# An SSM mixer layer with a dense and low-rank layer behind it on one core: x turned on VectorE and through DRAM instead of on TensorE, and the carried sum moved to GpSimd

## The chip, the cores and the metric

The kernel runs on one core of one Trainium2 chip. The metric is the device time of one execution in microseconds.

## What is computed

Input `x` is (2, 512, 512): batch, sequence, features. The reference, cut to what matters here:

```python
proj = einsum('bsd,ed->bse', layernorm(x), in_proj_w)       # gate 8192, x B C 10240, dt 128
hBC  = silu(causal_conv4(proj[..., INTER:INTER + CONV_DIM]) + conv_b)
hs, Bm, Cm = split(hBC)                                       # 128 heads of 64; 8 groups of 128 states
dt   = clip(softplus(dt + dt_bias), 0, 100);  xch = hs * dt[..., None]      # in chunks of 128 tokens
Y_diag = einsum('bzlhn,bzshn,bhzls,bzshp->bzlhp', Cc, Bc, L, xch)
states = einsum('bzlhn,bhzl,bzlhp->bzhpn', Bc, decay_states, xch)           # and carried over the chunks
Y_off  = einsum('bzlhn,bzhpn,bhzl->bzlhp', Cc, prev, exp(A_cum))
y = Y_diag + Y_off + hs * D;   g = y * silu(gate);   gg = g * rsqrt(mean(g * g) + EPS) * norm_w
x = x + einsum('bsi,oi->bso', gg, out_proj_w)
x = x + layernorm(x) @ W.T + b + sum_e probs_e * (layernorm(x) @ A_e.T) @ B_e.T
```

## The kernel before

The inner width of 8192 is cut into 64 units of 128 features, that is, two heads; eight units share one group's B and C. Features lie on the partitions after the projection, tokens on the free axis (two batches of 512 tokens). `body(g, last)` of each engine is a written-out loop over the eight units `j` of a group, and `k` counts the units. The engines are kept in step by counting semaphores, and each runs its instructions in the order written.

One unit on TensorE, in this order: the later half of the previous output product (`later_outs`), the projection of the next unit's x into `x_bank` (L778 to L780, each product in three parts of high and low halves), `states` for both batches (L786), `diagonal` (L797), the projection of the next unit's gate into `g_bank`, `carry` (L804), the first half of the output product (L835 to L837), in units 4 and 5 the projection of the next group's B or C, and `turn_hs` (L812): eight transposes that bring the next unit's x from features to tokens on the partitions, into `head_bank`.

```python
def turn_hs(k, s, b):
    pe.wait_ge(hs_ready, k + 1)
    reached(pe, carry_scaled, BATCH * (k - 1) + b + 1)
    for c in range(CHUNKS):
        mm = pe.transpose(head_bank[b][:, c * P:(c + 1) * P], hs[:, s, b, c * P:(c + 1) * P], ident[:])
    mm.then_inc(turned, 1)
```

The causal convolution of x has four taps: `tap0` is ScalarE's (L1033, `x_bank` to `hs`), the three others VectorE's (L1199), then Silu on ScalarE (L1045) makes `hs_ready`. VectorE's order in a unit: `to_heads` (L1278, the turned x times dt into `xdt`), `add_outs` and `score` in turns, `y_low_part` (L1215), in units 1 to 3 from the second group on `normed_out` (L1304), the first tap, `carried_state` (L1240, L1245), two taps, `skip` (L1261, which makes `y`), `carry_part` (L1256, both batches), `add_carry` (L1268, both batches, which adds the carried part to `y` and signals `y_sum`), and `add_outs`. In units 5 and 6 three taps of B or C (L1208) stand near its start, and in unit 7 `keep_bc` (L1285) ahead of `y_low_part`.

GpSimd multiplies `y` by the gate (`gated`, L1462, one instruction per batch, after `y_sum`) and `xdt` by the decay (`decayed`, L1469, after `xdt_ready`, and `states` on TensorE waits for it), and makes low halves (L1448, L1487) and the sum of squares (L1456). SyncE's queue issues every load: weights (L674), `out_raw` (L678), `scores` (L682) and, last in a unit, `grown_rows` (`load_grown`, L689, two DMAs per batch), which wait for that batch's `y_sum` because `carry_part` and `add_carry` use `grown_rows`.

## Time and profile before

| | |
|---|---|
| time, median of 3 runs | 1605.14 us (1604.95 to 1605.45) |
| the profiled execution, span | 1605.0 us |
| TensorE busy | 1583.5 us (99%) |
| VectorE busy | 1264.2 us (79%) |
| ScalarE busy | 1163.1 us (72%) |
| GpSimd busy | 700.7 us (44%) |
| DMA moved | 162.37 MB, 101 GB/s on average |

The page gives the span of the one profiled execution, and no time of it beside that. Busy shares are averages over the span; the order of things inside a unit is read from the timeline, where times count from the span's start. A TensorE matmul's duration contains its pipeline, so the step from one start to the next says what it costs.

### The profile page before, as it was taken

How to read it: one execution, taken by the hardware profiler on the slowest of the kernel's cores; microseconds unless marked ns; L12 is line 12 of the kernel's file. 1: busy time of each engine (PE TensorE's matmuls, PEld its weight loads, DVE VectorE, ACT ScalarE, POOL GpSimd, SP SyncE). 2: the span in 40 equal slices, each digit the busy share in tenths (PEclk: the TensorE clock that was granted, in tenths of full speed). 3: DMA queues.
4: the chain of work that ended last, by engine and by line, in shares of the span. 5: the costliest groups of instructions: out<-in, count | busy, mean ns of one | idle time of the engine just before them, and what ended most of it. 6: DMA issues, size and time to landing. Idle time of an engine off the chain costs nothing.

```text
span 1605.0 us, 26714 instructions
## 1 busy us (share of the span) xinstructions
PE 1583.5 (99%) x9576; PEld 1346.1 (84%) x9576; DVE 1264.2 (79%) x1984; ACT 1163.1 (72%) x2027; POOL 700.7 (44%) x535
## 2 busy tenths in 40 slices
PE   7899999999999999999999999999999999999998
PEld 5688888888888888888888888888888888888887
DVE  6687777877778777887778877787877878788787
ACT  5887667776777677777687766777677767777753
POOL 2155444453444454354453544445344445435550
PEclk9999999999999999999999999999999999999999
DMA  4542322332323233332232232233232323223211
GB/s 151 192 145 86 122 89 83 112 112 73 112 97 114 73 109 95 98 106 92 99 108 97 86 122 89 83 112 112 73 112 99 113 73 109 99 92 112 93 44 53
DMA packets 86916, 162.37 MB, mean 101 GB/s; under 512 B 23040, under 2 KB 39424, under 8 KB 86528
## 3 DMA queue, kind: packets, MB, share of 16 engines
q1 hardware_dynamic: 86784, 160.66, 30.8%
q8 instruction: 77, 1.26, 0.3%
q14 instruction: 55, 0.45, 0.1%
HBM read 154.84 MB, written 5.77 MB: 100 GB/s over the span
## 4 chain that ended last, share of the span: by engine, by line
PE 97%; DVE 1%; ACT 1%; issue 0%; DMA 0%; SPq 0%; DVEq 0%; ACTq 0%
PE g_bank L778 10%; PE g_bank L780 9%; PE g_bank L779 9%; PE d_bank L797 7%; PE x_bank L778 7%; PE x_bank L780 7%; PE x_bank L779 7%; PE head_bank L786 5%; PE head_bank L804 5%; PE x_bank L836 4%; PE x_bank L837 4%; PE x_bank L835 4%; PE d_bank L837 4%; PE d_bank L835 4%; PE d_bank L836 4%; PE head_bank L812 3%
## 5 line engine op out<-in xcount | busy, mean ns | idle before, releaser
L1448 POOL TENSOR_TENSOR w_low<-raw,w_high 128x512 fp32r<-128x512 f32 x139 | 179.8, 1294 | 553.5 <-ACT w_high L1011 553.5
L1199 DVE SCALAR_TENSOR_TENSOR hs<-x_bank,cols,hs 128x1022 f32<-128x1022 f32 x189 | 241.6, 1278 | 129.7 <-ACT hs L1033 127.5
L1021 ACT ACTIVATE scores<-scores,tables 128x128 f32<-128x128 f32 x1024 | 312.4, 391 | 0.0
L1462 POOL TENSOR_TENSOR y<-y,gate 128x512 f32<-128x512 f32 x128 | 185.4, 1467 | 198.8 <-DVE y L1268 198.8
L1033 ACT ACTIVATE hs<-x_bank,cols 128x1024 f32<-128x1024 f32 x63 | 75.9, 1204 | 269.9 <-PE x_bank L780 269.9
L778 PE MATMUL g_bank<-x_high,w_high 128*128 128x512 f32 x624 | 250.8, 402 | 0.0
L779 PE MATMUL g_bank<-x_low,w_high 128*128 128x512 f32 x624 | 243.2, 390 | 0.0
L780 PE MATMUL g_bank<-x_high,w_low 128*128 128x512 f32 x624 | 243.1, 390 | 0.0
L778 PE MATMUL x_bank<-x_high,w_high 128*128 128x512 f32 x504 | 196.3, 390 | 0.1
L780 PE MATMUL x_bank<-x_high,w_low 128*128 128x512 f32 x504 | 196.1, 389 | 0.0
L779 PE MATMUL x_bank<-x_low,w_high 128*128 128x512 f32 x504 | 196.1, 389 | 0.0
L1231 DVE TENSOR_TENSOR scores<-scores,bc 128x1024 f32<-128x1024 f32 x128 | 169.0, 1327 | 4.3 <-ACT scores L1026 4.3
L778 PEld LDWEIGHTS g_bank<-x_high,w_high 128*128 128x128 f32 x624 | 117.0, 188 | 33.4 <-issue 11.0
L1469 POOL TENSOR_TENSOR xdecay<-xdt,tables 128x384 f32<-128x384 f32 x128 | 109.0, 873 | 78.4 <-DVE xdt L1278 78.4
L780 PEld LDWEIGHTS g_bank<-x_high,w_low 128*128 128x128 f32 x624 | 117.1, 188 | 25.3
L1026 ACT ACTIVATE scores<-scores 128x1024 f32<-128x1024 f32 x128 | 135.8, 1062 | 2.6
L779 PEld LDWEIGHTS g_bank<-x_low,w_high 128*128 128x128 f32 x624 | 117.2, 188 | 22.4 <-issue 0.2
L1456 POOL TENSOR_TENSOR square_sum<-square_sum,gate 128x1024 f32<-128x1024 f32 x55 | 133.0, 2419 | 3.3 <-DVE scores L1231 2.9
L1245 DVE SCALAR_TENSOR_TENSOR state<-state,chunk_tab,head_bank 128x64 f32<-128x64 f32 x512 | 121.0, 278 | 9.1
L797 PE MATMUL d_bank<-scores,xdt 128*64 128x128 f32 x2048 | 126.1, 276 | 0.0
L1256 DVE TENSOR_TENSOR grown_rows<-head_bank,grown_rows 128x384 f32<-128x384 f32 x128 | 71.4, 557 | 64.4 <-PE head_bank L804 57.3
L797 PEld LDWEIGHTS d_bank<-scores,xdt 128*64 128x64 f32 x2048 | 110.5, 137 | 7.9 <-issue 0.2
(211 smaller groups left out, 3433.3 us busy)
## 6 DMA issues: line engine op xcount, KB each, us to landing
scores<-sums_dram SPq DMA_DIRECT2D x128, 512.0 KB, 4.8
raw<-w_in SPq DMA_DIRECT2D x144, 256.0 KB, 2.9
grown_rows<-grown_dram SPq DMA_DIRECT2D x256, 96.0 KB, 2.8
out_raw<-w_out SPq DMA_DIRECT2D x64, 256.0 KB, 3.4
mixed<-x SPq DMA_DIRECT2D x8, 256.0 KB, 5.1
out<-mixed SPq DMA_DIRECT2D x8, 256.0 KB, 2.0
table_dram<-table SPq DMA_DIRECT2D x2, 768.0 KB, 5.3
tables<-table_dram SPq DMA_DIRECT2D x30, 48.0 KB, 2.7
```

What stands on the lines that cost most here:

```text
L778: pe.matmul(to, w_high[:, slot, k], x_high[:, b, k], start=(k == 0), stop=False)
L779: pe.matmul(to, w_high[:, slot, k], x_low[:, b, k], start=False, stop=False)
L780: mm = pe.matmul(to, w_low[:, slot, k], x_high[:, b, k], start=False, stop=(k == KT - 1))
L797: mm = pe.matmul(d_bank[r * HEAD_DIM:(r + 1) * HEAD_DIM, b, c * P:(c + 1) * P], xdt[:, b, c, r], scores[:, s, b, r, c], start=True, stop=True)
L835: pe.matmul(to, y_high[:, q, b, at], out_high[:, q], start=(i == 0), stop=False)
L1021: op = s.activation(at, at, ACT.Relu, bias=col[:, r, c:c + 1], scale=-1.0)
L1026: s.activation(scores[:, q % 2, b], scores[:, q % 2, b], ACT.Exp, scale=-1.0).then_inc(exp_ready, 1)
L1199: v.scalar_tensor_tensor(out=hs[:, q % 2, :, i:], in0=x_bank[:, :, 0:SEQ - i], scalar=cols[:, q, TAPS - 1 - i:TAPS - i], in1=hs[:, q % 2, ...
L1231: v.tensor_tensor(at, at, bc[:, b].rearrange("p c l -> p (c l)").unsqueeze(1) .to_broadcast([P, PAIR, SEQ]), ALU.mult).then_inc(scores_rea ...
L1448: pool.tensor_tensor(w_low[:, slot], raw[:, slot], w_high[:, slot].bitcast(F32), ALU.subtract)\
L1456: pool.tensor_tensor(square_sum[:], square_sum[:], gate[:, q % 2], ALU.add).then_inc(square_added, 1)
L1462: pool.tensor_tensor(y[:, b], y[:, b], gate[:, q % 2, b], ALU.mult).then_inc(y_ready, 1)
```

## The change

The x of every unit but the first is no longer turned on TensorE. VectorE transposes `hs` in blocks of 32x32, one instruction per batch (`turn_blocks`), the result is stored to `blocks_dram`, one DMA per batch (`store_blocks`), and four DMAs per batch of 32 partitions each read it back so that the blocks too are in transposed places (`load_heads`). `to_heads` multiplies this `blocks` tile by dt; since the order of the features inside a head's 64 is now by halves of 32, the dt table is held twice, as two of four kinds. `to_heads` stands after the scores in VectorE's order and not at the unit's start. `add_carry` is GpSimd's, ahead of each batch's `gated`. `bias_high` and `bias_low` lie in the tiles of `x_low` and `x_high`, and their making waits for the last projection. The core of the diff:

```diff
@@ -19,6 +19,9 @@
 KT = HID // P
 UNITS = INTER // GROUPS // P
 PAIR = P // HEAD_DIM
+BLOCK = 32
+KINDS = 4
+QUARTERS = P // BLOCK
 GH = HEADS // GROUPS
 HALF = UNITS // 2
 ALL = GROUPS * UNITS
...
@@ -156,7 +160,7 @@
         big = lambda name: sb(name, [P, BATCH, CHUNKS * P])
         dense, wd = sb("dense", [P, KT, HID]), sb("wd", [P, KT, HID])
         sums, grown = big("head_sums"), big("head_grown")
-        table = sb("table", [P, BATCH, 2 * GROUPS, 3, GH // 2 * CHUNKS])
+        table = sb("table", [P, BATCH, 2 * GROUPS, KINDS, GH // 2 * CHUNKS])
         la, lb = sb("la", [P, ER, HID]), sb("lb", [P, ER, HID])
         xn = sb("xn", [P, 2, HID])
         wdt = sb("wdt", [P, KT, P])
...
@@ -398,9 +402,14 @@
             def table_of(i):
                 b, kind = TABLES[i]
                 s.wait_ge(table_turned, i + 1)
-                s.activation(table[:, b, :, kind].rearrange("p g (h c) -> p c g h", c=CHUNKS),
-                             bank[4 + i % 2].rearrange("p (c g h) -> p c g h", c=CHUNKS, g=2 * GROUPS),
-                             ACT.Copy).then_inc(table_ready, 1)
+                src = bank[4 + i % 2].rearrange("p (c g h) -> p c g h", c=CHUNKS, g=2 * GROUPS)
+                if kind == 0:
+                    twice = table[:, b, :, 0:2].rearrange("p g k (h z c) -> p z c g (k h)", z=2, c=CHUNKS)
+                    s.activation(twice[:, 0], src, ACT.Copy)
+                    s.activation(twice[:, 1], src, ACT.Copy).then_inc(table_ready, 1)
+                else:
+                    s.activation(table[:, b, :, 1 + kind].rearrange("p g (h c) -> p c g h", c=CHUNKS), src, ACT.Copy)\
+                        .then_inc(table_ready, 1)
 
             def first_tables(b):
                 s.wait_ge(table_ready, len(TABLES))
...
@@ -610,6 +619,7 @@
         square_sum, y = sb("square_sum", [P, BATCH, SEQ]), sb("y", [P, BATCH, SEQ])
         gate = sb("gate", [P, 2, BATCH, SEQ])
         out_raw = sb("out_raw", [P, 2, HID])
+        blocks = sb("blocks", [P, BATCH, QUARTERS, CHUNKS, BLOCK])
         xdt = sb("xdt", [P, BATCH, CHUNKS, PAIR, HEAD_DIM])
         c_feat, bc = sb("c_feat", [P, BATCH, SEQ]), sb("bc", [P, BATCH, CHUNKS, P])
         grown = grown_rows
...
@@ -660,6 +672,10 @@
 
         def table_of(kind, b, q):
             return tables[:, b, q // HALF, kind, PAIR * (q % HALF):PAIR * (q % HALF + 1)]
+
+        def dt_of(b, q):
+            twice = tables[:, b, q // HALF, 0:2].rearrange("p k h c -> p (k h) c")
+            return twice[:, QUARTERS * (q % HALF):QUARTERS * (q % HALF + 1)]
 
         (first_sync, first_stores, first_dense, first_gpsimd, first_tensor, first_scalar, first_vector,
          dense_ready) = first
...
@@ -688,6 +704,22 @@
                 for r in range(PAIR):
                     sp.dma_start(grown[r * HEAD_DIM:(r + 1) * HEAD_DIM, b].rearrange("p c l -> p (c l)"),
                                  rows[r, P:].partition_broadcast(HEAD_DIM)).then_inc(grown_in[b], 16)
+
+            def store_blocks(k):
+                for b in range(BATCH):
+                    sp.wait_ge(blocks_ready, BATCH * (k - 1) + b + 1)
+                    reached(sp, heads_in[b], 16 * QUARTERS * (k - 2))
+                    sp.dma_start(blocks_dram[BATCH * (k % 2) + b], blocks[:, b].rearrange("p j n f -> p (j n f)"))\
+                      .then_inc(blocks_stored[b], 16)
+
+            def load_heads(k):
+                for b in range(BATCH):
+                    sp.wait_ge(blocks_stored[b], 16 * k)
+                    turned_blocks = blocks_dram[BATCH * (k % 2) + b].rearrange("(q t) (j n) -> j t q n", t=BLOCK,
+                                                                               j=QUARTERS)
+                    for i in range(QUARTERS):
+                        sp.dma_start(blocks[i * BLOCK:(i + 1) * BLOCK, b].rearrange("p q n f -> p q (n f)"),
+                                     turned_blocks[i]).then_inc(heads_in[b], 16)
 
             def load_chunks(g, b, half):
                 at = slice(half * GH // 2, (half + 1) * GH // 2)
...
@@ -744,8 +776,10 @@
                     for at in splits[2:]:
                         load_weight(*at)
                     if ahead:
+                        store_blocks(ahead[2])
                         for b in range(BATCH):
                             load_grown(ahead[2], b)
+                        load_heads(ahead[2])
                     if last and j == UNITS - 1:
                         sp.wait_ge(b_turned, BATCH * GROUPS)
                         sp.dma_start(bias_row, bias.partition_broadcast(P)).then_inc(bias_in, 16)
...
@@ -782,6 +816,7 @@
 
             def states(k, b):
                 pe.wait_ge(xdecay_ready, BATCH * k + b + 1)
+                reached(pe, carry_scaled, BATCH * (k - 1) + b + 1)
                 for c in range(LATER):
                     mm = pe.matmul(head_bank[b][:, c * P:(c + 1) * P], b_tok[:, b, c],
                                    xdecay[:, b, c].rearrange("p r d -> p (r d)"), start=True, stop=True)
...
@@ -805,11 +840,10 @@
                                    c_feat[:, b, (c + 1) * P:(c + 2) * P], start=True, stop=True)
                 mm.then_inc(carried, 1)
 
-            def turn_hs(k, s, b):
-                pe.wait_ge(hs_ready, k + 1)
-                reached(pe, carry_scaled, BATCH * (k - 1) + b + 1)
+            def turn_first(b):
+                pe.wait_ge(hs_ready, 1)
                 for c in range(CHUNKS):
-                    mm = pe.transpose(head_bank[b][:, c * P:(c + 1) * P], hs[:, s, b, c * P:(c + 1) * P], ident[:])
+                    mm = pe.transpose(head_bank[b][:, c * P:(c + 1) * P], hs[:, 0, b, c * P:(c + 1) * P], ident[:])
                 mm.then_inc(turned, 1)
 
             def bc_of(b, to):
...
@@ -937,9 +971,6 @@
                         pe.wait_ge(gate_ready, BATCH * (k + 2))
                         for b in range(BATCH):
                             project(g, (NEXT_B, NEXT_C)[j - 4], b, g_bank[:, b])
-                    if ahead:
-                        for b in range(BATCH):
-                            turn_hs(k + 1, (j + 1) % 2, b)
                     if j == 0 and g > 0:
                         pe.wait_ge(square_added, (UNITS - 1) * g)
                         pe.wait_ge(gate_ready, BATCH * (k + 2))
...
@@ -1157,6 +1188,7 @@
                     if last and j == UNITS - 1:
                         s.activation(ident_r[:], ident[:], ACT.Copy)
                         s.wait_ge(bias_in, 16)
+                        s.wait_ge(projected, BATCH * TILES)
                         s.activation(bias_high[:], bias_row, ACT.Copy).then_inc(bias_high_ready, 1)
                         s.wait_ge(dense_in, 16)
                         for i in range(KT):
...
@@ -1261,23 +1293,31 @@
                 v.scalar_tensor_tensor(out=y[:], in0=hs[:, q % 2], scalar=d_col[:, q:q + 1], in1=d_bank[:],
                                        op0=ALU.mult, op1=ALU.add).then_inc(skip_added, 1)
 
-            def add_carry(k, b):
-                u = BATCH * k + b
-                v.wait_ge(carry_scaled, u + 1)
-                v.wait_ge(skip_added, k + 1)
-                v.tensor_tensor(y[:, b, P:], y[:, b, P:], grown[:, b].rearrange("p c l -> p (c l)"), ALU.add)\
-                 .then_inc(y_sum, 1)
+            def turn_blocks(k, i):
+
+                v.wait_ge(hs_ready, k + 1)
+                for b in range(BATCH):
+                    reached(v, blocks_stored[b], 16 * (k - 1))
+                    v.transpose(blocks[:, b], hs[:, i, b].rearrange("p (c j t) -> p j c t", j=QUARTERS, t=BLOCK))\
+                     .then_inc(blocks_ready, 1)
 
             def to_heads(g, q, k, b):
                 if q % HALF == 0:
                     v.wait_ge(tables_in[b][q // HALF], 16 * (g + 1))
-                v.wait_ge(turned, BATCH * k + b + 1)
                 reached(v, diag_done, BATCH * (k - 1) + b + 1)
                 reached(v, xdecay_ready, BATCH * (k - 1) + b + 1)
-                col = table_of(DT, b, q).rearrange("p r c -> p c r")
-                v.tensor_tensor(xdt[:, b], head_bank[b].rearrange("p (c r d) -> p c r d", c=CHUNKS, r=PAIR),
-                                col.unsqueeze(3).to_broadcast([P, CHUNKS, PAIR, HEAD_DIM]), ALU.mult)\
-                 .then_inc(xdt_ready, 1)
+                if k == 0:
+                    v.wait_ge(turned, b + 1)
+                    col = dt_of(b, q)[:, 0::QUARTERS // PAIR].rearrange("p r c -> p c r")
+                    v.tensor_tensor(xdt[:, b], head_bank[b].rearrange("p (c r d) -> p c r d", c=CHUNKS, r=PAIR),
+                                    col.unsqueeze(3).to_broadcast([P, CHUNKS, PAIR, HEAD_DIM]), ALU.mult)\
+                     .then_inc(xdt_ready, 1)
+                else:
+                    v.wait_ge(heads_in[b], 16 * QUARTERS * k)
+                    v.tensor_tensor(xdt[:, b].rearrange("p c r (h f) -> p (r h) c f", f=BLOCK),
+                                    blocks[:, b],
+                                    dt_of(b, q).unsqueeze(3).to_broadcast([P, QUARTERS, CHUNKS, BLOCK]), ALU.mult)\
+                     .then_inc(xdt_ready, 1)
 
             def keep_bc(g, src):
                 v.wait_ge(bc_product, BATCH * (g + 1))
...
@@ -1359,8 +1399,9 @@
                     k = UNITS * g + j
                     prev, now, ahead = (unit(g, last, j + i) for i in range(-1, 2))
 
-                    for b in range(BATCH):
-                        to_heads(g, j, k, b)
+                    if k == 0:
+                        for b in range(BATCH):
+                            to_heads(g, j, k, b)
                     if j == 1 and g > 0:
                         squares_of(g)
                     if k > 2:
...
@@ -1375,6 +1416,9 @@
                         add_outs(g, j - 1, (3,))
                     if scores_here:
                         score(g, j, k, 1)
+                    if k > 0:
+                        for b in range(BATCH):
+                            to_heads(g, j, k, b)
                     if j == UNITS - 1 and not last:
                         keep_bc(g + 1, g_bank)
                     if prev and ahead:
...
@@ -1392,17 +1436,15 @@
                         tap(2, *ahead)
                         tap(3, *ahead)
                         skip(j, k)
+                        turn_blocks(k + 1, (j + 1) % 2)
                         for b in range(BATCH):
                             carry_part(k, b)
-                        for b in range(BATCH):
-                            add_carry(k, b)
                     else:
                         y_low_part(prev[1], prev[2])
                         v.wait_ge(y_low_ready, k)
                         skip(j, k)
                         for b in range(BATCH):
                             carry_part(k, b)
-                            add_carry(k, b)
                     if k > 1:
                         add_outs(g, j, (0, 1))
                     else:
...
@@ -1455,6 +1497,13 @@
                 reached(pool, square_added, (UNITS - 1) * g + q - 1)
                 pool.tensor_tensor(square_sum[:], square_sum[:], gate[:, q % 2], ALU.add).then_inc(square_added, 1)
 
+            def add_carry(k, b):
+                u = BATCH * k + b
+                pool.wait_ge(skip_added, k + 1)
+                pool.wait_ge(carry_scaled, u + 1)
+                pool.tensor_tensor(y[:, b, P:], y[:, b, P:], grown[:, b].rearrange("p c l -> p (c l)"), ALU.add)\
+                    .then_inc(y_sum, 1)
+
             def gated(q, k, b):
                 u = BATCH * k + b
                 pool.wait_ge(y_sum, u + 1)
...
@@ -1489,6 +1538,7 @@
                     for at in splits[1:]:
                         low_part(*at)
                     for b in range(BATCH):
+                        add_carry(k, b)
                         gated(j, k, b)
 
             low_part(0, 3)
...
```

SyncE's queue, a plain unit of the kernel before, the named tiles being those of the loads above:

```order
L674 DMA raw<-w_in 128x512
L682 DMA scores<-sums_dram 128x1024 x2
L689 DMA grown_rows<-grown_dram 64x384 x4
L674 DMA raw<-w_in 128x512
L678 DMA out_raw<-w_out 128x512
```

The same place in the change:

```order
L690 DMA raw<-w_in 128x512
L698 DMA scores<-sums_dram 128x1024 x2
L712 DMA blocks_dram<-blocks 128x512 x2
L705 DMA grown_rows<-grown_dram 64x384 x4
L721 DMA blocks<-blocks_dram 32x4x128 x8
L690 DMA raw<-w_in 128x512
L694 DMA out_raw<-w_out 128x512
```

The two stores stand ahead of the four loads of `grown_rows`, the eight loads behind them and ahead of the next unit's weights.

VectorE, unit 1 of a group from its scores on, in the change (L1317 is `to_heads`, L1263 `score`, L1344 `normed_out`, L1301 `turn_blocks`, L1288 `carry_part`):

```order
L1263 TENSOR_TENSOR scores<-scores,bc 128x1024
L1317 TENSOR_TENSOR xdt<-blocks,tables 128x4x4x32 x2
L1247 SCALAR_TENSOR_TENSOR y_low<-y,cols,y_high 128x1024
L1363 RECIPROCAL g_rstd<-g_std 128x8
L1344 SCALAR_TENSOR_TENSOR mixed<-acc,g_rstd,mixed 128x512 x2
L1231 SCALAR_TENSOR_TENSOR hs<-x_bank,cols,hs 128x2x511
L1272 COPY state<-head_bank 128x128
...
L1293 SCALAR_TENSOR_TENSOR y<-hs,cols,d_bank 128x1024
L1301 STREAM_TRANSPOSE blocks<-hs 128x512 x2
L1288 TENSOR_TENSOR grown_rows<-head_bank,grown_rows 128x384 x2
L1340 TENSOR_TENSOR acc<-x_bank,acc 128x512 x2
```

`to_heads` has moved from the unit's start to behind the scores, ahead of `y_low_part`, the normed sums and the first tap; the two block transposes stand where the two `add_carry` stood behind `carry_part`, but ahead of it.

GpSimd, the end of a unit in the change (L1504 is `add_carry`, L1511 `gated`, L1518 `decayed`):

```order
L1490 TENSOR_TENSOR w_low<-raw,w_high 128x512
L1504 TENSOR_TENSOR y<-y,grown_rows 128x384
L1511 TENSOR_TENSOR y<-y,gate 128x512
L1504 TENSOR_TENSOR y<-y,grown_rows 128x384
L1511 TENSOR_TENSOR y<-y,gate 128x512
L1518 TENSOR_TENSOR xdecay<-xdt,tables 128x384 x2
```

Before, the four rows in the middle were one, `y<-y,gate` twice; the second batch's sum now comes behind the first batch's gate.

## Rows read from the trace of the kernel before

**Rows 1.** The page: busy us (share) xinstructions; shares of the chain that ended last, by engine

```profile
PE 1583.5 (99%) x9576; PEld 1346.1 (84%) x9576; DVE 1264.2 (79%) x1984; ACT 1163.1 (72%) x2027; POOL 700.7 (44%) x535
...
PE 97%; DVE 1%; ACT 1%; issue 0%; DMA 0%; SPq 0%; DVEq 0%; ACTq 0%
```

**Rows 2.** The waits: engine line <- released by: us in total, times, longest

```profile
DVE hs L1199 <- ACT hs L1033: 127.5, 62, 3.3
```

**Rows 3.** Timeline of ScalarE, `tap0`: start, us, line, [idle before <- releaser]

```profile
892.73 1.21 ACT L1033 ACTIVATE hs<-x_bank,cols 128x1024 f32<-128x1024 f32 x1 [4.80 <-PE x_bank L780]
...
914.73 1.21 ACT L1033 ACTIVATE hs<-x_bank,cols 128x1024 f32<-128x1024 f32 x1 [4.75 <-PE x_bank L780]
...
969.69 1.20 ACT L1033 ACTIVATE hs<-x_bank,cols 128x1024 f32<-128x1024 f32 x1 [4.75 <-PE x_bank L780]
...
993.57 1.21 ACT L1033 ACTIVATE hs<-x_bank,cols 128x1024 f32<-128x1024 f32 x1 [4.80 <-PE x_bank L780]
...
1016.21 1.20 ACT L1033 ACTIVATE hs<-x_bank,cols 128x1024 f32<-128x1024 f32 x1 [3.92 <-PE x_bank L780]
...
1039.12 1.20 ACT L1033 ACTIVATE hs<-x_bank,cols 128x1024 f32<-128x1024 f32 x1 [3.13 <-PE x_bank L780]
...
1083.26 1.21 ACT L1033 ACTIVATE hs<-x_bank,cols 128x1024 f32<-128x1024 f32 x1 [4.80 <-PE x_bank L780]
```

**Rows 4.** Timeline of TensorE around the transposes of one unit

```profile
905.00 0.39 PE L836 MATMUL x_bank<-out_low,y_high 128*128 128x512 f32 x1
905.23 0.39 PE L837 MATMUL x_bank<-out_high,y_low 128*128 128x512 f32 x1
905.46 1.03 PE L812 MATMUL head_bank<-ident,hs 128*128 128x128 f32 x8
906.25 0.48 PE L835 MATMUL d_bank<-out_high,y_high 128*128 128x512 f32 x1
```

**Rows 5.** Timeline of VectorE over the same units

```profile
890.56 2.07 DVE L1304 SCALAR_TENSOR_TENSOR mixed<-acc,g_rstd,mixed 128x512 f32<-128x512 f32 x3
893.97 1.28 DVE L1199 SCALAR_TENSOR_TENSOR hs<-x_bank,cols,hs 128x1022 f32<-128x1022 f32 x1 [1.34 <-ACT hs L1033]
...
900.10 1.27 DVE L1261 SCALAR_TENSOR_TENSOR y<-hs,cols,d_bank 128x1024 f32<-128x1024 f32 x1
902.25 1.23 DVE L1256 TENSOR_TENSOR grown_rows<-head_bank,grown_rows 128x384 f32<-128x384 f32 x2 [0.88 <-PE head_bank L804]
903.40 1.02 DVE L1268 TENSOR_TENSOR y<-y,grown_rows 128x384 f32<-128x384 f32 x2
...
906.27 1.28 DVE L1278 TENSOR_TENSOR xdt<-head_bank,tables 128x512 f32<-128x512 f32 x2
...
911.41 1.27 DVE L1215 SCALAR_TENSOR_TENSOR y_low<-y,cols,y_high 128x1024 fp32r<-128x1024 f32 x1
...
925.44 1.62 DVE L1268 TENSOR_TENSOR y<-y,grown_rows 128x384 f32<-128x384 f32 x2
...
990.39 1.23 DVE L1285 TENSOR_TENSOR bc<-g_bank,causal 128x1024 f32<-128x1024 f32 x1
```

**Rows 6.** Timeline of GpSimd in that unit

```profile
904.02 2.79 POOL L1462 TENSOR_TENSOR y<-y,gate 128x512 f32<-128x512 f32 x2 [3.33 <-DVE y L1268]
907.03 1.64 POOL L1469 TENSOR_TENSOR xdecay<-xdt,tables 128x384 f32<-128x384 f32 x2 [0.21 <-DVE xdt L1278]
```

**Rows 7.** Timeline of SyncE's DMA queue in that unit

```profile
903.97 2.37 SPq L689 DMA_DIRECT2D grown_rows<-grown_dram  x4
```

**Rows 8.** DMA issues (ns min/median/max) and landing: L674; L689 and its landing; a store

```profile
L674 SPq DMA_DIRECT2D raw<-w_in x138: 327/333/1240, 55.0 to 1489.4; - x138
...
L689 SPq DMA_DIRECT2D grown_rows<-grown_dram x252: 444/596/1980, 82.7 to 1543.5; - x126
...
DMA to landing us min/median/max: 2.5/2.8/5.1
...
sums_dram<-head_sums SPq DMA_DIRECT2D x2, 256.0 KB, 2.5
```

19 lines of the change are left out of this document (11 added, 8 removed).

## The prediction

> **What bounds the kernel now.** I began with the busy shares and the chain of work that ended last: TensorE is busy 99% of the span and carries 97% of that chain, no other engine over 79% [rows 1]. So time taken off TensorE is time off the kernel, as long as nothing else comes to hold it. The next view is the waits: VectorE waits 127.5 us in 62 units, about 2 us each, for ScalarE's `tap0`, which itself follows TensorE's projection [rows 2]. That is all the slack VectorE has, and in the units with normed sums it is less. The starts of `tap0` mark the units: a plain one takes 22.0 us (892.73 to 914.73), the two with a B or C projection 55.0 together, the next three 23.9, 22.6 and 22.9, and two more 44.1; eight units 190.5 [rows 3].
>
> **What TensorE loses.** Between two matmuls of the output product the starts lie 0.23 apart; with the eight transposes of L812 between them it is 905.23 to 906.25, so they take 0.8 us [rows 4]. They go in 63 units (only the first keeps them): 63 x 0.8 = 50 us, which with everything else hidden gives 1605.0 - 50 = 1555. The plain unit would be 21.2 us.
>
> **What comes in its place.** The transposes' result came from PSUM within a microsecond. Now it comes by this path, in a loop that closes once per unit: first tap, carried states, taps, skip, two block transposes, carry multiplication (VectorE); add, gate, add (GpSimd); the second batch's `grown` loads, eight block loads (SyncE's queue); landing; `xdt`, `y_low`, normed sums, and the next unit's first tap (VectorE). It is in one piece because `load_heads` stands behind both batches of `load_grown`, which wait for `y_sum` of both batches, and that sum is now GpSimd's, behind the first batch's gate multiplication. I add it up in the unit that starts at 893.97:
> - First tap to the end of skip: 893.97 to 901.3, 7.35 us (skip starts at 900.10 and takes 1.27, of which the next instruction overlaps some 0.07) [rows 5]. `hs` has its Silu by then.
> - Two transposes: no row shows this operation. The nearest are 128x512 on VectorE: `xdt`, two in 1.28 us [rows 5]. I take 1.25 for both; from below 0.6 (twice the rate), from above 2.5 (half the rate).
> - `grown` of batch 0: 1.23 for two, so 0.6 [rows 5]. Batch 1's is hidden behind GpSimd.
> - GpSimd: the gate multiplication of 128x512 takes 1.4 (two in 2.79), and `xdecay`, 384 wide, 0.82 (two in 1.64) [rows 6]. An add of 384 plain elements I take as 0.95; bounds 0.8 and 1.4. Add, gate, add with the handoffs: 3.35. On VectorE the two adds took 1.02 [rows 5], so VectorE's total stays as it was: 1.25 on, 1.0 off.
> - SyncE: four `grown` issues take 2.37 us, 0.59 each; batch 1's two: 1.2 [rows 7]. Then eight block loads, seven issues before the last one starts. Weight loads over 128 partitions issue in 0.33, `grown` over 64 partitions in 0.60 (medians) [rows 8]. A block load has 32 partitions and 512-byte pieces. The partial-partition row is nearest, so I take 0.6: 4.2 us. The low end is 0.33 (2.3 us), the high end 1.0 if pieces of 512 bytes queue up (7 us).
> - Landing: 2.8 us for `grown`, of 96 KB [rows 8]; a block load has 64 KB. I take 2.8; from below 2.2, from above 5, the longest of `grown` being 5.1.
> - `xdt` of batch 1 0.65, then `y_low` 1.2 [rows 5].
> The sum is 7.35 + 1.25 + 0.6 + 3.35 + 1.2 + 4.2 + 2.8 + 0.65 + 1.2 = 22.6 us, against TensorE's 21.2. The two stores are not in it: issued at about 902 and, with 2.5 us as for `sums_dram` [rows 8], landed by 905, while the SyncE queue stands at `y_sum` until about 906.5. Behind the eight loads wait the next weight and `out_raw` loads, whose data are used a unit later: nothing. ScalarE gets `y` about 1 us later, which comes out of the 3.1 to 4.8 us that it idles before `tap0` [rows 3]: nothing.
>
> The same loop closes through TensorE: `xdecay` of batch 1 ends 0.85 after its `xdt`, some 23.5 us after the start of `tap0`; TensorE would want it 0.7 after the start of `states`, at about 21.6. So the stall should stand in front of `states` (L786 of the kernel before).
>
> **The Trainium skill against this.** The row says 2.8 us for a small load. *DMA: Bandwidth & Descriptors*, section "Anatomy of one DMA", gives 2.0 us plus the bytes at 436 GB/s (for DMAs issued from GpSimd), an estimated 2.15 us for 64 KB; by it the loop would be 21.95 and the time 1613. The trace's row is longer, so I stay with the row. The same page's "Rules for kernel authors" says that transfers to separate parts of the partitions serialise and are better one transfer; it speaks against four loads where one would do, and no row here shows such a split by four.
>
> **Sum over eight units.** Each takes the larger of TensorE's time and the loop's.
> - Three units have normed sums, behind `xdt` in VectorE's queue and so in the loop: three of them take 2.07 us [rows 5], two with the reciprocal about 1.6. Times 24.2, 24.7, 24.7 (22.9, 22.05, 22.05 before).
> - The plain unit: 22.6 (22.0 before).
> - The two with extra projections: TensorE 27.5 - 0.8 = 26.7 each. The loop has 4 us to spare there.
> - The one after: the causal product, 1.23 [rows 5], follows `xdt`: 23.7 (23.9 before).
> - The last: 22.6 (22.6 before).
> Together 195.9 against 190.5, +5.4. Seven groups: +38. The first group has no normed sums and comes out even. The doubled `dt` table adds two ScalarE copies in the prologue and the last unit's sum goes over GpSimd, +1 together. **Forecast: 1605.0 + 39 = 1644 us.** The profiled span, 1605.0, is 0.1 under the median of the runs, 1605.14, so nothing is corrected. A measurement here can tell 0.2%, 3.2 us, from no change.
>
> **Rivals.**
> 1. *The loads issue fast.* At 0.43 each, the loop is 21.4: units of 23.0, 23.5, 23.5, 21.4, 26.7, 26.7, 23.1 and 21.9, together 189.8, so -0.7 in seven groups and -6 in the first: 1595. At 0.33 and 2.2 us to landing it is 20.1, the plain units are TensorE's, and the sum is 186.1: 1569. For it: the weight loads' 0.33 [rows 8]. Against: `grown`, with fewer pieces than these, takes 0.6. It decides below about 0.45 us per issue. This is the case on the other side. Chance 0.24.
> 2. *All hidden*, TensorE stays the bound everywhere: 1555. It needs the loop with normed sums under 21.2, 3.5 us less than the above. Chance 0.03.
> 3. *The transfers queue up* or the block transpose runs at half rate: a loop of 24.1 (1.5 more, say 0.8 us per load) gives 25.7, 26.2, 26.2, 24.1, 26.7, 26.7, 25.2 and 24.1, together 204.9: +14.4 in seven groups and 9 in the first, 1715. For it: GpSimd and VectorE read SBUF together, and one pair of adds took 1.62 instead of 1.02 [rows 5]. Chance 0.15.
> 4. *The change does not do what it says*, and the transposes stay: excluded by the instruction order, where they are gone from TensorE. A time within 0.2% comes about only where the loop happens to lie near 21.6: 0.08.
> The forecast itself, 1615 to 1680, has 0.50.
>
> **The numbers.** Slower by over 0.2%: the forecast's 0.50 and rival 3's 0.15, 0.65. Same: 0.08. Faster: 0.24 and 0.03, 0.27. The range takes in rival 1's low end nearly, 1575, and most of rival 3, 1700.
>
> **What would show it.** TensorE's busy time shorter by about 50 us and yet not the span: new idle time in front of `states`, released by GpSimd's `xdecay`, 1 to 3 us per unit, in five or six units of eight, and none in the two with extra projections. VectorE should wait for the landing of `blocks`. SyncE's queue should show eight issues of about 0.6 us that start right after `grown`. I am wrong if issues take 0.45 or less, if `heads_in` is met before VectorE gets to `xdt`, or if `states` waits for nothing.

## The result and the profile after

The changed kernel takes 1738.13 us (median of 4 runs, 1735.61 to 1740.38) against 1605.3: 1.0823 of the time before (95% interval 1.0808 to 1.0839), 133 us slower. The direction was forecast, with 1644 us; the size was not, and the time lies above the range. The profiled span is 1735.6 us.

The page, busy shares and the chain that ended last by engine, where rows 1 stood before:

```profile
PE 1593.1 (92%) x9072; PEld 1331.0 (77%) x9072; DVE 1353.4 (78%) x1982; ACT 1165.9 (67%) x2029; POOL 932.1 (54%) x663
...
PE 28%; issue 21%; DVE 19%; POOL 16%; SPq 8%; DMA 4%; ACT 3%; POOLq 0%; DVEq 0%; ACTq 0%
```

TensorE is busy 92% of the span and carries 28% of the chain where it carried 97%; VectorE, GpSimd, SyncE's queue and DMA now make up nearly half of it (47%), and much of the "issue" share lies between their links. The waits:

```profile
ACT hs L1064 <- PE x_bank L814: 167.2, 52, 4.8
...
PEld head_bank L821 <- POOL xdecay L1518: 140.1, 91, 4.9
PE head_bank L821 <- POOL xdecay L1518: 114.1, 91, 4.5
DVE xdt L1317 <- DMA blocks<-blocks_dram: 104.8, 71, 3.9
...
DVE grown_rows L1288 <- PE head_bank L839: 57.7, 35, 4.2
```

The stall stands where the prediction put it: `states` (L821 now) waits for `xdecay`, 91 times, 114 us in TensorE's matmuls, and VectorE waits 105 us for the block loads. The last row is a wait that the forecast's loop has not: `carry_part` on VectorE waits for TensorE's `carry` up to 4.2 us, because TensorE, after a stall, comes to it late. The kernel before has the same wait 63 times, never over 0.9 us. The chain over one turn of the loop, start, us and what:

```profile
975.23 1.01 POOL y L1504
...
976.32 0.08 POOL y L1511
...
977.56 1.02 POOL y L1504
...
978.60 0.45 SPq L705
...
979.73 0.58 SPq L721
...
983.20 2.00 DMA blocks<-blocks_dram
...
985.32 0.70 DVE xdt L1317
...
986.10 1.82 POOL xdecay L1518
...
987.96 1.65 PE head_bank L821 x6
```

That is the forecast path, link by link: add, gate (of which the chain shows only the start; the rest is in an "issue" piece), add, `grown`, eight block loads, landing, `xdt`, `xdecay`, `states`. The loads themselves, issue in ns and landing in us, min/median/max:

```profile
L721 SPq DMA_DIRECT2D blocks<-blocks_dram x504: 303/432/1729, 89.0 to 1672.6; - x168
...
DMA to landing us min/median/max: 1.8/2.0/3.3
```

A block load issues in 0.43 us and lands 2.0 after that, not 0.6 and 2.8. By the prediction's own list this is a sign of being wrong (issues of 0.45 or less). The block transpose cost what was taken for it, 0.62 each start to start:

```profile
L1301 DVE STREAM_TRANSPOSE blocks<-hs x126: 667/692/715, 81.6 to 1662.0; 128x512 f32<-128x512 f32 x126
```

So the loop without the normed sums is shorter than forecast: first tap to first tap 966.00 to 987.13, 21.1 us, where 22.6 was forecast. VectorE over this stretch, and before it the normed sums (L1344) of the unit ahead:

```profile
959.11 1.28 DVE L1247 SCALAR_TENSOR_TENSOR y_low<-y,cols,y_high 128x1024 fp32r<-128x1024 f32 x1
960.30 5.77 DVE L1344 SCALAR_TENSOR_TENSOR mixed<-acc,g_rstd,mixed 128x512 f32<-128x512 f32 x3
966.00 1.27 DVE L1231 SCALAR_TENSOR_TENSOR hs<-x_bank,cols,hs 128x1022 f32<-128x1022 f32 x1
...
973.33 1.31 DVE L1301 STREAM_TRANSPOSE blocks<-hs 128x512 f32<-128x512 f32 x2
...
985.93 1.28 DVE L1247 SCALAR_TENSOR_TENSOR y_low<-y,cols,y_high 128x1024 fp32r<-128x1024 f32 x1
987.13 1.27 DVE L1231 SCALAR_TENSOR_TENSOR hs<-x_bank,cols,hs 128x1022 f32<-128x1022 f32 x1
```

Three normed sums took 5.77 us; the same three took 2.07 before [rows 5]. GpSimd at the same time:

```profile
957.34 0.84 POOL L1518 TENSOR_TENSOR xdecay<-xdt,tables 128x384 f32<-128x384 f32 x1 [3.41 <-DVE xdt L1317]
959.27 1.81 POOL L1518 TENSOR_TENSOR xdecay<-xdt,tables 128x384 f32<-128x384 f32 x1 [1.09 <-DVE xdt L1317]
961.04 1.72 POOL L1490 TENSOR_TENSOR w_low<-raw,w_high 128x512 fp32r<-128x512 f32 x1
962.73 2.79 POOL L1498 TENSOR_TENSOR square_sum<-square_sum,gate 128x1024 f32<-128x1024 f32 x1
965.48 1.73 POOL L1536 TENSOR_TENSOR out_low<-out_raw,out_high 128x512 fp32r<-128x512 f32 x1
967.17 1.30 POOL L1490 TENSOR_TENSOR w_low<-raw,w_high 128x512 fp32r<-128x512 f32 x1
```

The two engines' instructions follow one another here. The second `xdecay` starts at 959.27 beside `y_low` and takes 1.81 instead of 0.84; it ends at 961.08. The first normed sum, begun at 960.30, takes 1.33 us and ends 0.55 after that; the weight's low part, begun at 961.04, takes 1.72 instead of 1.29; the second normed sum ends 0.55 after it, having taken 1.76, and the third, beside the sum of squares, takes 2.83, to 966.07. Over the whole kernel, L1344:

```profile
L1344 DVE SCALAR_TENSOR_TENSOR mixed<-acc,g_rstd,mixed x64: 739/1543/2880, 295.0 to 1721.5; 128x512 f32<-128x512 f32 x64
```

Before it took 741 ns on average, and GpSimd was idle at that place (it had been for 7.9 us when its next low part started at 894.54). Last, the granted TensorE clock, the seventh column of the windows (the window, its length, busy us of TensorE, its weight loads, VectorE, ScalarE, GpSimd, then the clock, DMA share and GB/s):

```profile
931.00:956.50 25.50, 21.69 (x129) 17.80 (x127) 21.59 (x29) 16.17 (x30) 15.67 (x9) 1.00 0.35 113
956.50:984.80 28.30, 24.57 (x128) 20.51 (x128) 23.59 (x31) 16.22 (x30) 16.23 (x11) 0.88 0.41 133
984.80:1015.70 30.90, 28.63 (x152) 23.91 (x152) 22.76 (x32) 18.09 (x32) 16.79 (x12) 0.94 0.36 115
```

In the stretches that hold the long stalls and follow them, the mean clock is 0.88 to 0.94, that is, part of them at 1.2 GHz and the rest at 2.4; over the run it is 0.967 against 0.998 before. The `diagonal` of a unit, 32 products, takes 3.68 us at 962.72 in the timeline of TensorE and 2.76 at 989.54, against 1.97 at full clock (1018.60). An estimate from the means: at a share of 0.967, TensorE's clock gave 57 us less than full speed over the span of 1735.6 us; before, 3 us (0.998 of 1605.0). That is not all lost time, since some of it falls where TensorE is not waited for, but it is too much to be left out of an account of 133 us.

The steps between starts of `tap0`, in us, show where the time goes (a column names the two units in whose loop bodies they stand, and the first one is unit 7 to unit 0; a group of the middle of the run, each from the timeline of ScalarE):

| kernel | 7-0 | 0-1 | 1-2 | 2-3 | 3-4 | 4-5 | 5-6 | 6-7 | sum |
|---|---|---|---|---|---|---|---|---|---|
| before | 22.6 | 22.9 | 22.0 | 22.1 | 22.0 | 27.5 | 27.5 | 23.9 | 190.5 |
| forecast | 22.6 | 24.2 | 24.7 | 24.7 | 22.6 | 26.7 | 26.7 | 23.7 | 195.9 |
| the change | 21.8 | 23.6 | 21.8 | 25.4 | 28.3 | 30.9 | 28.2 | 24.7 | 204.8 |
| with GpSimd waiting | 21.8 | 23.7 | 21.8 | 23.1 | 23.7 | 29.1 | 28.3 | 24.7 | 196.0 |
| block loads first | 21.8 | 22.2 | 21.2 | 22.1 | 24.9 | 27.3 | 28.2 | 24.7 | 192.5 |
| the last kernel below | 21.8 | 22.0 | 21.1 | 21.2 | 21.1 | 26.6 | 26.6 | 23.0 | 183.4 |

The same starts over the whole run say where the 94 us above the forecast of 1644 lie: the first group is 19 us longer than forecast, the six middle groups (204.3 to 208.1 each, for 195.9) together 59, the last 8, and what follows its last `tap0` 7.

### The profile page after: what moved, and what is told of

It is laid out like the page before. It is cut to its first block, busy times and chain, and to the rows that moved or that the text cites. A ratio compares the mean times of both kernels' runs of the same rounds, so it can differ in the third digit from the quotient of the medians.

```text
span 1735.6 us, 26642 instructions
## 1 busy us (share of the span) xinstructions
PE 1593.1 (92%) x9072; PEld 1331.0 (77%) x9072; DVE 1353.4 (78%) x1982; ACT 1165.9 (67%) x2029; POOL 932.1 (54%) x663
## 4 chain that ended last, share of the span: by engine, by line
PE 28%; issue 21%; DVE 19%; POOL 16%; SPq 8%; DMA 4%; ACT 3%; POOLq 0%; DVEq 0%; ACTq 0%
POOL y L1504 8%; SPq L721 6%; DVE mixed L1344 5%; POOL xdecay L1518 5%; PE d_bank L832 4%; PE g_bank L812 4%; PE g_bank L813 4%; PE g_bank L814 4%; DMA blocks<-blocks_dram 4%; DVE hs L1231 3%; POOL y L1511 3%; DVE state L1277 3%; PE head_bank L821 2%; DVE y L1293 2%; SPq L705 2%
## 5 line engine op out<-in xcount | busy, mean ns | idle before, releaser
L1518 POOL TENSOR_TENSOR xdecay<-xdt,tables 128x384 f32<-128x384 f32 x128 | 166.8, 1308 | 369.5 <-DVE xdt L1317 359.3
L1504 POOL TENSOR_TENSOR y<-y,grown_rows 128x384 f32<-128x384 f32 x128 | 151.6, 1184 | 250.9 <-DVE grown_rows L1288 250.9
L821 PE MATMUL head_bank<-xdecay,b_tok 128*128 128x128 f32 x768 | 126.7, 308 | 114.1 <-POOL xdecay L1518 114.1
L821 PEld LDWEIGHTS head_bank<-xdecay,b_tok 128*128 128x128 f32 x768 | 107.1, 208 | 142.4 <-POOL xdecay L1518 140.1
L1511 POOL TENSOR_TENSOR y<-y,gate 128x512 f32<-128x512 f32 x128 | 195.1, 1524 | 10.0
L1263 DVE TENSOR_TENSOR scores<-scores,bc 128x1024 f32<-128x1024 f32 x128 | 182.5, 1433 | 1.2 <-ACT scores L1057 1.2
L1076 ACT ACTIVATE hs<-hs 128x1024 f32<-128x1024 f32 x64 | 67.9, 1062 | 161.5 <-DVE hs L1231 159.5
L1317 DVE TENSOR_TENSOR xdt<-blocks,tables 128x512 f32<-128x512 f32 x126 | 88.4, 711 | 111.3 <-DMA blocks<-blocks_dram 104.8
L832 PE MATMUL d_bank<-scores,xdt 128*64 128x128 f32 x2048 | 151.8, 311 | 0.0
L832 PEld LDWEIGHTS d_bank<-scores,xdt 128*64 128x64 f32 x2048 | 134.6, 158 | 9.1 <-issue 2.9
```

The lines of the kernel that those rows point to most:

```text
L821: mm = pe.matmul(head_bank[b][:, c * P:(c + 1) * P], b_tok[:, b, c], xdecay[:, b, c].rearrange("p r d -> p (r d)"), start=True, stop=True)
L832: mm = pe.matmul(d_bank[r * HEAD_DIM:(r + 1) * HEAD_DIM, b, c * P:(c + 1) * P], xdt[:, b, c, r], scores[:, s, b, r, c], start=True, stop=True)
L1263: v.tensor_tensor(at, at, bc[:, b].rearrange("p c l -> p (c l)").unsqueeze(1) .to_broadcast([P, PAIR, SEQ]), ALU.mult).then_inc(scores_rea ...
L1504: pool.tensor_tensor(y[:, b, P:], y[:, b, P:], grown[:, b].rearrange("p c l -> p (c l)"), ALU.add)\
L1511: pool.tensor_tensor(y[:, b], y[:, b], gate[:, q % 2, b], ALU.mult).then_inc(y_ready, 1)
L1518: pool.tensor_tensor(xdecay[:, b], xdt[:, b, 0:LATER], col.unsqueeze(3).to_broadcast([P, LATER, PAIR, HEAD_DIM]), ALU.mult)\
```

## Experiments

Theory S: a loop through VectorE, GpSimd, SyncE's queue and DRAM is the bound, and it is lengthened where VectorE and GpSimd instructions that both read two SBUF tensors fall together and take turns. Rivals: L, the loop's length alone; T, TensorE's lower clock; D, the latency of the trip through DRAM itself. No run holds the stalls and changes the clock, so with the gains of the single edits stands the mean clock of the run.

**Normed sums ahead of `to_heads`.**

```diff
+                    if j == 1 and g > 0:
+                        group_rstd(g)
+                    if g > 0:
+                        for at in {1: (0, 1), 2: (2, 3, 4), 3: (5, 6, 7)}.get(j, ()):
+                            normed_out(g, at)
                     if k > 0:
                         for b in range(BATCH):
                             to_heads(g, j, k, b)
...
-                    if j == 1 and g > 0:
-                        group_rstd(g)
-                    if g > 0:
-                        for at in {1: (0, 1), 2: (2, 3, 4), 3: (5, 6, 7)}.get(j, ()):
-                            normed_out(g, at)
```

> The change, with group_rstd and the normed sums moved ahead of to_heads in VectorE's order, so that they lie in the time in which VectorE waits for the block loads. Theory S (the loop through DRAM, plus VectorE and GpSimd instructions that serialise when both read two SBUF tensors; three normed sums took 5.8 us instead of 2.07 beside GpSimd's work): the normed sums leave the loop and meet a nearly idle GpSimd, 740 to 900 ns each again, and seven groups lose some 12 us each: 1640 to 1665. Theory L (only the loop's length counts, the slow normed sums cost no more than their 2.07 us would): 7 x 5.7 = 40 us less, 1695 to 1700. Theory T (TensorE's lower clock is what costs): 1720 or more.

Measured 1682.8 us, 55 less than the change (mean clock 0.986 for 0.967). The normed sums are short again (groups by line, busy us and mean ns):

```profile
L1344 DVE SCALAR_TENSOR_TENSOR mixed<-acc,g_rstd,mixed 128x512 f32<-128x512 f32 x64 | 44.8, 746 | 0.3
```

The gain lies between the two figures, so of itself it decides neither; L's 40 is passed, and S's price was too high, since `to_heads` is held back by the 2 us that the sums take.

**A wait more on GpSimd.** Only this is added, and nothing is taken away:

```diff
+                    if g > 0 and j in (1, 2, 3):
+                        pool.wait_ge(mixed_ready, TB * (g - 1) + (2, 5, 8)[j - 1])
                     for at in splits[:1]:
                         low_part(*at)
```

> The change, with one wait added on GpSimd in units 1 to 3: its low parts and sums of squares start only after the unit's normed sums. The loop's instructions and their order stay. Theory S: the three normed sums take about 2.1 to 2.9 us instead of 5.8 (only the second xdecay can still meet them), the units with them lose 3 us each, about 6 us in a group, 7 groups: 1695 +- 8, though an instruction was only delayed and nothing was taken away. Theory L: no change or slower, 1738 to 1745.

Measured 1678.6 us, 59 us faster than the change, by a wait; S had priced it at 1695 +- 8 and the gain was 16 us larger. VectorE, `y_low` and the normed sums:

```profile
932.39 1.28 DVE L1247 SCALAR_TENSOR_TENSOR y_low<-y,cols,y_high 128x1024 fp32r<-128x1024 f32 x1
933.58 2.65 DVE L1344 SCALAR_TENSOR_TENSOR mixed<-acc,g_rstd,mixed 128x512 f32<-128x512 f32 x3
```

GpSimd, the second `xdecay` and, after a wait of 1.95 us, the low part:

```profile
932.55 1.81 POOL L1518 TENSOR_TENSOR xdecay<-xdt,tables 128x384 f32<-128x384 f32 x1 [1.12 <-DVE xdt L1317]
936.31 1.29 POOL L1490 TENSOR_TENSOR w_low<-raw,w_high 128x512 fp32r<-128x512 f32 x1 [1.95 <-DVE mixed L1344]
```

Three sums took 2.65 us. This is what settles it for S: the order and the loop are the same, and only the overlap is gone. L is refuted (it allowed no gain). T cannot be what starts it, for nothing was done here to the clock, and it rose to 0.984 with shorter stalls. But it can add to what a stall costs: by the estimate above, 27 us of clock are missing here and 57 in the change, so up to 30 of the 59 us may have come back by way of the clock. How much of them did is not shown.

**Block loads ahead of the `grown` loads.**

```diff
                         store_blocks(ahead[2])
+                        load_heads(ahead[2])
                         for b in range(BATCH):
                             load_grown(ahead[2], b)
-                        load_heads(ahead[2])
```

> The change, with load_heads ahead of load_grown in SyncE's order, so that the block loads wait for the stores alone and not for y_sum of both batches. The path turn, store 0.3 and landing 2.0, eight loads 3.4 and landing 2.0 takes the place of carry, add, gate, add, grown, eight loads and landing: some 2.3 us less in every unit in which the loop is the bound. Theories S and L alike: 40 to 90 us less than the change, 1650 to 1700, and the stall in front of states falls by about half; S adds that the normed sums stay at over 1.2 us each. A rival, that the latency of the DRAM trip itself is the bound: less than 15 us gained.

Measured 1629.0 us, 109 less, more than was expected. TensorE's wait (weight loads and matmuls) falls to less than half:

```profile
PEld head_bank L821 <- POOL xdecay L1518: 61.3, 68, 4.6
...
PE head_bank L821 <- POOL xdecay L1518: 41.8, 61, 4.2
```

D falls: the trip through DRAM is the same, VectorE's wait for its landing is gone (0.3 us in all, where it was 104.8), and what the trip cost was standing in the queue behind `y_sum`. The normed sums stay slow (mean 1364 ns), as S said. 2.3 us in five or six units of eight groups are 92 to 110 us, so 109 is not beyond that sum. Part of it may be the clock, whose mean rose to 0.995: by the estimate above some 8 us are missing here and 57 in the change. No run separates the two.

**The carried sum back on VectorE**, the rest of the change kept.

```diff
                         turn_blocks(k + 1, (j + 1) % 2)
                         for b in range(BATCH):
                             carry_part(k, b)
+                        for b in range(BATCH):
+                            add_carry(k, b)
...
-                        add_carry(k, b)
                         gated(j, k, b)
```

> The change with add_carry back on VectorE behind carry_part, all else as in the change. In the change y_sum of the second batch comes 3.1 us after carry_part has ended (add 1.0, gate 1.3, add 1.0 on GpSimd); on VectorE two adds take 1.0. The loop is 2.1 us shorter in each of the five or six units of a group in which it is the bound. Theory: 1738 - 8 x 5 x 2.1 = 1650, between 1640 and 1680. Rival, that GpSimd's part of the change is harmless, as it was in the kernel before (1607.1): 1725 or more.

Measured 1673.9 us (mean clock 0.981), inside the theory's range: 64 us of the 133 hang on the sum being GpSimd's, in this kernel. (The gains of these single edits, 55, 59, 109 and 64 us, overlap and do not add up to the 133.)

**The carried sum on GpSimd alone**, x turned by TensorE as before.

```diff
+                        add_carry(k, b)
                         gated(j, k, b)
```

VectorE's calls of it, not shown, are taken out.

> The kernel before, with only add_carry moved to GpSimd; x is still turned by TensorE and to_heads stays where it was. If the carried sum on GpSimd costs by being later (1.1 us) or by contention alone, it shows here: 1615 or more. If it costs only as a part of the loop through SyncE's queue, which this kernel does not have, TensorE stays the bound: 1605 +- 3, with adds of about 1.0 us on GpSimd.

Measured 1607.1 us against 1606.3 for the kernel before, ratio 1.0006 (0.9997 to 1.0016): the same. The add itself, mean 1.12 us beside 0.65 on VectorE:

```profile
L1452 POOL TENSOR_TENSOR y<-y,grown_rows 128x384 f32<-128x384 f32 x128 | 143.4, 1120 | 141.4 <-DVE grown_rows L1256 138.0 <-ACT gate L1053 3.4
```

The same edit costs nothing in one kernel and 64 us in the other, where SyncE's queue holds the block loads behind the sum. The queue is not all of it: with the block loads ahead of the `grown` loads, a later pair of runs still differs by 9 us.

**Loads first and normed sums early together.** Both diffs above.

> Block loads ahead of the grown loads and the normed sums ahead of to_heads, both together on the change. Block loads first gave 1629.0, with normed sums of 1364 ns each; the normed sums alone gave 55 us. If the two savings are of the same loop, only what is left over its bound can be saved again: 1600 to 1615. If they add in full: 1574. If heads-first had already taken the normed sums out of what bounds: 1625 or more.

Measured 1641.3 us, 12 us *slower* than loads first alone. The figure falls under the last case, 1625 or more, but no case said that the edit would cost time. With the loads in early, `to_heads` has no wait in which the normed sums could hide (0.3 us of waiting for loads in the whole run of loads first), and they come ahead of it with their 2 us; TensorE's weight loads wait longer:

```profile
PEld head_bank L821 <- POOL xdecay L1518: 81.5, 75, 4.6
```

**`to_heads` early.** Loads first; `to_heads` ahead of the second score and ahead of the taps of B and C; normed sums of units 2 and 3 ahead of it.

```diff
                     scores_here = last or j not in (5, 6)
                     if scores_here:
                         score(g, j, k, 0)
                     if k > 2:
                         add_outs(g, j - 1, (3,))
+                    if g > 0:
+                        for at in {2: (2, 3, 4), 3: (5, 6, 7)}.get(j, ()):
+                            normed_out(g, at)
+                    if k > 0:
+                        for b in range(BATCH):
+                            to_heads(g, j, k, b)
+                    if j in (5, 6) and not last:
+                        for i in range(1, TAPS):
+                            bc_tap(i, 2 * (g + 1) + j - 5, j - 5)
+                    if scores_here:
+                        score(g, j, k, 1)
```

The same calls are taken out where they stood.

> Block loads first, and to_heads ahead of the second score and, in units 5 and 6, ahead of the three taps of B or C; the normed sums of units 2 and 3 stand ahead of to_heads, those of unit 1 stay. The loads are in at about 17 us after tap0, and states would take xdecay at 21.6. Theory: the stall in front of states goes nearly everywhere, above all in units 5 and 6, where 1.5 us stood after block loads first; what remains is TensorE's own time: 1560 to 1585, faster than the kernel before. Rival, that VectorE has become the bound because its sums serialise with GpSimd's: 1595 or more, with no stall on landing loads.

Measured 1601.4 us, ratio 0.9985 (0.9969 to 1.0), level with before. The theory's 1560 to 1585 was missed, and the rival's figure, 1595 or more, came true, and nearly its sign: VectorE waits for the landing of blocks for only 5.0 us in the whole run. With `to_heads` ahead of the taps of B and C, the last three steps of a group fell from 27.3, 28.2 and 24.7 to 26.6, 26.6 and 23.0, TensorE's own times. What was left stood in steps 2-3 and 3-4, of 24.2 and 23.2. This is what VectorE had done in such a unit in the change, the taps of B or C (L1240) between a wait for TensorE and `to_heads`:

```profile
1008.90 0.69 DVE L1340 TENSOR_TENSOR acc<-d_bank,acc 128x512 f32<-128x512 f32 x1 [2.94 <-PE d_bank L871]
1009.51 3.90 DVE L1240 SCALAR_TENSOR_TENSOR bc_conv<-g_bank,tap_bc,bc_conv 128x1022 f32<-128x1022 f32 x3
...
1013.92 1.28 DVE L1317 TENSOR_TENSOR xdt<-blocks,tables 128x512 f32<-128x512 f32 x2
```

**The same with `add_carry` on VectorE**, behind both `carry_part`, and gone from GpSimd's loop:

```diff
                         for b in range(BATCH):
                             carry_part(k, b)
+                        for b in range(BATCH):
+                            add_carry(k, b)
```

> As the kernel with to_heads early, and add_carry back on VectorE. VectorE does 1.0 us more in a unit and GpSimd 2.0 less. If VectorE's order is what holds the loop: 5 to 20 us slower than the one with add_carry on GpSimd. If what counts is contention on GpSimd: 5 to 15 us faster than it. If TensorE is the bound in both: the same within 3 us.

Measured 1592.4 us, ratio 0.9914 (0.9898 to 0.993): 9 us faster than with the sum on GpSimd, as the second case had it (contention on GpSimd). VectorE in unit 2, normed sums, `xdt`, the second score and `y_low`:

```profile
877.10 2.07 DVE L1351 SCALAR_TENSOR_TENSOR mixed<-acc,g_rstd,mixed 128x512 f32<-128x512 f32 x3
879.09 1.29 DVE L1324 TENSOR_TENSOR xdt<-blocks,tables 128x512 f32<-128x512 f32 x2
880.29 1.22 DVE L1263 TENSOR_TENSOR scores<-scores,bc 128x1024 f32<-128x1024 f32 x1
881.42 1.86 DVE L1247 SCALAR_TENSOR_TENSOR y_low<-y,cols,y_high 128x1024 fp32r<-128x1024 f32 x1
```

and GpSimd's two `xdecay` beside them, 4.13 us where two took 1.64 [rows 6]:

```profile
879.85 4.13 POOL L1523 TENSOR_TENSOR xdecay<-xdt,tables 128x384 f32<-128x384 f32 x2 [5.29 <-DVE xdt L1324]
```

**Normed sums between the block transposes and `carry_part`.** On top of the last one:

```diff
                         turn_blocks(k + 1, (j + 1) % 2)
+                        if j == 1 and g > 0:
+                            group_rstd(g)
+                        if g > 0:
+                            for at in {1: (0, 1), 2: (2, 3, 4), 3: (5, 6, 7)}.get(j, ()):
+                                normed_out(g, at)
```

The earlier calls of both are taken out.

> As the kernel with to_heads early and add_carry on VectorE, with the normed sums of units 1 to 3 (and group_rstd) between the block transposes and carry_part, where VectorE waits 1.4 us for TensorE's carry and GpSimd is idle. There the two units with three normed sums took 23.2 us each with the sums ahead of to_heads, two xdecay in 4.1. Theory: the sums take 740 ns each, to_heads comes 2.0 us sooner in those units and they fall to 21.2 to 22, that is 7 x 2 x 1.2 to 2.0 = 17 to 28 us less than 1592: 1564 to 1575. Rival, that carry_part and y_sum then come late and move the stall elsewhere: 1585 or more.

Measured 1566.7 us, ratio 0.9756 (0.9742 to 0.9769), 26 us less, as the theory priced it.

**`to_heads` ahead of the fourth sum of the output product**, so that a sum that reads PSUM runs beside the first `xdecay`.

```diff
-                    if k > 2:
-                        add_outs(g, j - 1, (3,))
                     if k > 0:
                         for b in range(BATCH):
                             to_heads(g, j, k, b)
+                    if k > 2:
+                        add_outs(g, j - 1, (3,))
```

> As the one before, with to_heads also ahead of the fourth sum of the output product, so that the first xdecay runs beside an instruction that reads PSUM and not two SBUF tensors. Theory S (they serialise only when both read SBUF twice): the two xdecay of a unit take 3.0 us or less instead of 4.1, and a unit still bound by them gains up to 0.6 us: 0 to 20 us less than the one before. Rival, that the loads have not landed so early: VectorE waits for them and the time is 5 us or more above it.

Measured 1560.1 us, ratio 0.9716 (0.9702 to 0.9729): 7 us less again, and 2.8% faster than the kernel before. The gain is in the range, but of S's condition this run is weak evidence: one `xdecay` took 1287 ns on average where it took 1391 in the run before, a pair 2.6 us for 2.8, and the second one still meets a score. The page's busy line, then the groups of `xdecay` and of `states`:

```profile
PE 1527.8 (98%) x9072; PEld 1292.8 (83%) x9072; DVE 1362.6 (88%) x2110; ACT 1162.1 (75%) x2029; POOL 760.8 (49%) x535
```

```profile
L1521 POOL TENSOR_TENSOR xdecay<-xdt,tables 128x384 f32<-128x384 f32 x128 | 163.1, 1287 | 231.1 <-DVE xdt L1324 220.8 <-DVE xdt L1319 10.2
...
L821 PE MATMUL head_bank<-xdecay,b_tok 128*128 128x128 f32 x768 | 96.8, 275 | 3.8 <-POOL xdecay L1521 3.8
```

TensorE waits 3.8 us for `xdecay` in the whole run where it waited 114, and all eight steps of a group are within 0.2 us of TensorE's own time. This is the change's idea, x no longer turned on TensorE, worth 46 us with its order mended; its second half, the sum on GpSimd, is undone in it.

## Why the prediction was right and wrong

The mechanism was right in kind, a loop whose stall stands in front of `states`, and two things in its sum were not: the normed sums, put at 2.07 us in a place where they took 5.8, and the path itself, which left out TensorE's own part behind a stall and VectorE's wait in the units with extra projections. The cheaper loads pulled the other way. In detail:

- *The transposes take 0.8 us of TensorE per unit, 1555 if all else is hidden*: right. The last kernel reaches 1560.1, with steps of 21.1 and 26.6 where 21.2 and 26.7 were forecast for TensorE alone.
- *A loop takes their place, and the stall stands in front of `states`, released by `xdecay`*: right, link by link, for the links it names. What the path lacked is what TensorE does behind the stall: `states`, `diagonal`, the gate projection and `carry`, for which VectorE then waits up to 4.2 us (57.7 in all), part of it at 1.2 GHz. The sum has neither this wait nor a term for the clock.
- *Issue 0.6 and landing 2.8 of a block load*: wrong, 0.43 and 2.0. The plain loop is 21.1 and not 22.6 us. By this error alone the forecast would have been too slow; it is the condition of rival 1 (and the prediction's own sign of being wrong), and yet the kernel was slower.
- *Three normed sums take 2.07 in the loop*: the term that failed most. They took 5.8, since `to_heads` behind the scores brought them beside `xdecay` and the low parts, and both engines' instructions took turns. The kernel with GpSimd waiting puts this at 59 us of the 133, with what shorter stalls give back in clock. I had seen the sign of it, the pair of adds at 1.62, but named it under rival 3 beside a price of 1.5 us per unit that was meant for slow loads or transposes, and gave it none where it would fall.
- *The two units with extra projections are TensorE's, the loop has 4 us to spare*: wrong. `to_heads` there stands behind three taps of B or C in VectorE's queue (3.9 us), and ahead of these VectorE waits 2.9 us for a product of the output (`acc`), so that `to_heads` starts with no wait for the block loads, at 1013.92 in the unit shown; then two `xdecay` beside `y_low` take 3.0. The steps 5-6 and 6-7 were 28.2 and 24.7 and not 26.7 and 23.7, in every group but the last, which has no such projections in them. With `to_heads` ahead of the taps (and of the second score) they were 26.6 and 23.0.
- *The first group comes out even*: wrong. From the prologue's `tap0` to unit 8's it took 207.8 us against 189.0. Its second and third step were 18.2 and 18.6 us before, which no row of the prediction shows, and a loop of 22.6 there is 8 us more by the prediction's own rule. Measured, they were 20.1 and 24.2, and the next 28.2 for 22.1. In the last two of the three, which start at 92.7 and 116.9, the mean clock was 0.86 and 0.88, and no term of the sum had TensorE slower after its stalls, though the loop also passes through TensorE (`states` to `carry`). No run separates the clock's share in this group from the loop's; that stays open.
- *Each unit takes the larger of two times*: only nearly right. Units that miss TensorE's time hand their delay on: step 4-5 was 30.9 for a TensorE time of 26.7, after the slow normed sums of unit 3, in which a full turn of the loop (to `xdecay`'s end at 987.91) is followed by TensorE's own work. That the delay adds up like this is a reading of the chain; no run tests it by itself.
- *Rival 3, transfers that queue up*: they did not (0.43 and 2.0). Its 1715 was the nearest figure, and that is luck for its mechanism; the contention that it names beside them was there.

## What to carry to other kernels

When a step on the bound engine is replaced by a trip through other queues, look up what stands ahead of it in each queue: here the block loads stood behind a load that had to wait for an unrelated sum, and one moved line gave back 109 us. Before an instruction is moved or an engine is given more to do, ask which instruction of the other engine it will run beside, since two of them may each be fast and take turns; a wait that keeps them apart can be a gain. A move that is free in one kernel (the sum on GpSimd, 1607.1 us) is not free in another: what counts is what waits behind it. And where the bound engine begins to stall, look at its clock in the same stretch: the stalls and the lower clock come together.

## What the hardware showed that was not expected

- VectorE and GpSimd instructions that both read two tensors from SBUF took turns: a normed sum of 741 ns took up to 2880 ns and an `xdecay` of 0.84 us took 1.81. With GpSimd made to wait, three normed sums fell from 5.77 to 2.65 us. Beside VectorE's taps, which read one tensor from PSUM, GpSimd's low part took 1.28 us, its usual time.
- An SBUF to DRAM store of 256 KB landed 2.0 us after its issue, a load of 64 KB in pieces of 512 bytes 2.0, less than the 2.7 of `grown_rows`, whose pieces are larger.
- TensorE's granted clock fell in stretches with waits of 2 to 5 us in front of `states`, to means of 0.88 to 0.94. At unit 3 of the group shown TensorE waited 2.58 us, ran 0.94 and waited 1.97 (958.23 to 961.14), and a window set over 960.5 to 967.3 has a clock of 0.50, the one from 967.4 to 987.7 a clock of 1.00.
